# A four-layer graph network kernel: the loop without the transposes of Gd

## The chip, the cores and the metric

The kernel runs on one core of a Trainium2 chip. The metric is the device time of one execution in microseconds (us); less is better. The engines are TensorE (PE, with its weight loads as PEld), VectorE (DVE), ScalarE (ACT), GpSimd (POOL) and SyncE (SP), whose queue issues the DMAs.

## The reference

There are 128 graphs of 128 nodes with 256 features. Each passes four layers in turn, and after each layer the state is normalized over its features. The first layer is the one that the change touches (cut to its core):

```python
H = (adj != 0).astype(x.dtype)
w = adj.reshape(N, -1)[:, :C]
xw = einsum('ncd,hd->nch', x, W)
Dn = einsum('nce,ne->nc', H, w);  Dn = where(Dn > 0, 1.0 / Dn, 0.0)
Be = H.sum(axis=1);               Be = where(Be > 0, 1.0 / Be, 0.0)
m = Be[:, :, None] * einsum('nce,nch->neh', H, xw)
out = Dn[:, :, None] * einsum('nce,neh->nch', H, m) + b
# layer 1: y = conv(layer_norm(relu(conv(x, W1))), W2) + x;  x = layernorm(x + y)
# layer 2: x = layernorm(x + relu([x, adj @ x / deg] @ W));  layer 3: three GCN steps with adj
# layer 4: x = layernorm(x + relu((adj @ x) @ K) * (x has a nonzero))
```

So one convolution multiplies the state by diag(Dn) H diag(Be) H^T. The product G = H diag(Be) H^T is symmetric.

## The kernel before, in words

The work goes by pairs of graphs, 64 of them; g = 0, 1 is the graph in the pair, C = 128 the nodes, D = 256 the features. Each pair passes stages with short names, each a group of matmuls on PE and what the other engines do with its result. Products that need the full precision are taken as high and low parts (`_hi`, `_lo`): ACT rounds a value to its high part, and DVE or POOL subtracts that from the value to get the low part (`low_...` in the code); three matmuls then stand for one.

The stages of a pair around the change:

- `G(p)`: two matmuls make H diag(Be) H^T, the part with Be's high half in columns 0 to 127 and that with its low half in 128 to 255, and the degree Dn's sum in the last two columns.
- `scale_G(p)` on DVE: adds the two sums of the degree, inverts it (`dinv`, one number per node and graph, lying down the partitions), and makes Gd = dinv * (high half + low half), row by row, in three instructions: Gl (L1670), then Gd for each g (L1674).
- `Tr(p)` on PE (L417): two transposes of Gd, since the matmuls want it transposed. `copy_GT` on ACT copies the result from PSUM to GT, `round_GT` rounds it to GT_hi, and `low_GT` on POOL makes GT_lo.
- `Gx(p)`: GT by x. `R(p, 0)`, `R(p, 1)`: by W1. `P(p, 0)`, `P(p, 1)`: by W2, with `squares(p)` for the norm over the 512 hidden features. `square_mean`, `wide_var`, `root_h` and `make_p` (ACT, DVE, ACT, DVE) turn that norm into p; `round_p` and `low_p` split it. `GP(p)`: GT's parts by p's parts. `sum_n1` and `make_x1` then make the state of layer 2, which `xT` transposes.

The other stages (XAB, AXB; Ax2, H1, H1W, H2, H2W, AP3; Ax3, TK) are layers 2 to 4. Every engine runs one written list: `fill` for pairs 0 to 6, then `body(n)` for n = 7 to 61 (55 times), then `drain`. A body works on a different pair in each layer: n for G, Gd and Gx, n-1 for R, P and GP, n-2 to n-5 further down. On PE a body goes

```python
R(n-1,0) R(n-1,1) G(n) xT(n-2) H2W(n-4) Ax2(n-3) XAB(n-2) H1(n-3) AP3(n-4) P(n-1,0) P(n-1,1)
squares(n-1) Tr(n) AXB(n-2) H1W(n-3) Ax3(n-4) Gx(n) H2(n-3) GP(n-1) TK(n-4)
```

Nothing reorders this at run time: an instruction that waits on a semaphore holds all that stand behind it on its engine. SP's body loads the input of pair n+2 and stores the output of pair n-5, in that order. PSUM bank 0 is used by Ax2, Tr, H2 and R1 in turn.

Of the kernel before, what the change touches and what calls it, by code (L numbers as in the profile page):

```python
# [5 lines left out]
F32 = mybir.dt.float32  # L6
# [40 lines left out]
def build(nc, x, adjT, w1T, w2T, wab, v1, v2, v3, wk, columns, rows, eye, out):  # L47
# [5 lines left out]
    with ExitStack() as ctx:  # L53
# [70 lines left out]
        class Norm:  # L124
# [13 lines left out]
            def mv(self, p):  # L138
# [11 lines left out]
        table_loaded = sem("table_loaded")  # L150
        consts_step, beta_made, w1_hi, w1_lo, w2_scaled, w2_mean, w2_centred, w2c_hi, w2c_lo = (
            sem(s) for s in ("consts_step", "beta_made", "w1_hi", "w1_lo", "w2_scaled", "w2_mean",
                             "w2_centred", "w2c_hi", "w2c_lo"))
        betaW_made, wab_hi, wab_lo, v_hi, v_lo, b2_made = (
# [5 lines left out]
            sem(s) for s in ("ht_made", "ht_counted", "be_max", "be_made", "be_hi", "be_lo", "bh_high", "bh_made"))  # L160
        dn_0, dn_1, dn_2, dn_3, gl_made, gd_made = (sem(s) for s in ("dn_0", "dn_1", "dn_2", "dn_3", "gl_made", "gd_made"))
        w_hi, w_lo, gt_made, gx_hi, gx_lo = (sem(s) for s in ("w_hi", "w_lo", "gt_made", "gx_hi", "gx_lo"))
# [126 lines left out]
        def _(sp):  # L289
# [80 lines left out]
        def _(pe):  # L370
# [68 lines left out]
            def P(p, h):  # L439
                if p == 0 and h == 0:  # L440
                    pe.wait_ge(w2c_lo, 1)
# [154 lines left out]
            def fill():  # L596
# [10 lines left out]
                pe.wait_ge(gt_hi, 1)  # L607
                pe.wait_ge(w2_mean, 1)
                G(2)
# [174 lines left out]
            def body(n):  # L784
# [23 lines left out]
                squares(n - 1)  # L808
                pe.wait_ge(ax2_lo, n - 2)
                Tr(n)  # L810
                AXB(n - 2)
# [5 lines left out]
                Gx(n)  # L817
                pe.wait_ge(gt_hi, n + 1)
                H2(n - 3)
# [169 lines left out]
        def _(act):  # L989
# [63 lines left out]
            def copy_GT(p):  # L1053
                act.wait_ge(pe_did["Tr"], upto(p))
                if begun(p - 2):
                    act.wait_ge(pe_did["Gx"], upto(p - 2))
                    act.wait_ge(gt_lo, upto(p - 2))
                copy(GT[p % 2][:].rearrange("p a b -> p (a b)"),
                     psum[:, bank("Tr", p), 0:2 * C]).then_inc(gt_made, 1)

            def round_GT(p):
                if begun(p - 2):
                    act.wait_ge(pe_did["GP"], upto(p - 2))
                copy(GT_s[p % 2][0][:].rearrange("p a b -> p (a b)"),
                     psum[:, bank("Tr", p), 0:2 * C]).then_inc(gt_hi, 1)
# [136 lines left out]
            def round_w2():  # L1202
                act.wait_ge(w2_centred, 1)
                copy(w2c_s[0][:, :, 0:D], w2g[:]).then_inc(w2c_hi, 1)

# [178 lines left out]
            def body(n):  # L1384
# [178 lines left out]
        def _(dve):  # L1563
# [90 lines left out]
            def scale_G(p):  # L1654
                b = bank("G", p)
                both = slice(b[0], b[1] + 1, b[1] - b[0])
                dn = psum[:, b[1], 2 * C + 2:2 * C + 4]
                dve.wait_ge(pe_did["G"], upto(p))
                dve.tensor_reduce(dn, psum[:, both, 2 * C:2 * C + 2], AX_X, ALU.add).then_inc(dn_0, 1)
                dve.wait_ge(dn_0, upto(p))  # L1660
                dve.tensor_scalar(dn_max[:], dn, TINY, None, ALU.max).then_inc(dn_1, 1)
                dve.wait_ge(dn_1, upto(p))
                dve.reciprocal(dn_inv[:], dn_max[:]).then_inc(dn_2, 1)
                dve.wait_ge(dn_2, upto(p))
                dve.scalar_tensor_tensor(out=dinv[:], in0=dn, scalar=0.0, in1=dn_inv[:],
                                         op0=ALU.is_gt, op1=ALU.mult).then_inc(dn_3, 1)
                dve.wait_ge(dn_3, upto(p))
                if begun(p - 1):
                    dve.wait_ge(pe_did["Tr"], upto(p - 1))
                dve.tensor_tensor(Gl[:], psum[:, both, C:2 * C], bc(dinv[:], [C, 2, C], 2),  # L1670
                                  ALU.mult).then_inc(gl_made, 1)
                dve.wait_ge(gl_made, upto(p))
# [49 lines left out]
            def node_degree(p):  # L1722
                b = bank("AXB", p)
                dve.wait_ge(pe_did["AXB"], upto(p))
                dve.tensor_scalar(degm[:], psum[:, b:b + 2, D], DEG_EPS, None, ALU.max).then_inc(deg_max, 1)
                dve.wait_ge(deg_max, upto(p))
                dve.reciprocal(rdeg[:], degm[:]).then_inc(deg_inv, 1)

            def make_agg(p):
                b = bank("AXB", p)  # L1730
                dve.wait_ge(xa_out, upto(p))
                dve.wait_ge(deg_inv, upto(p))
# [37 lines left out]
            def mean_w2():  # L1770
                dve.wait_ge(pe_did["W2"], 1)
                dve.tensor_scalar(w2mean[:], psum[:, bank("W2", 0), 0:D], 1.0 / DH, None, ALU.mult).then_inc(w2_mean, 1)

            def centre_w2():
                dve.wait_ge(w2_mean, 1)
                dve.wait_ge(w2_scaled, KH)
                dve.tensor_tensor(w2g[:], w2g[:], bc(w2mean[:], [C, KH, D], 1), ALU.subtract).then_inc(w2_centred, 1)

            def high_w2():
                dve.wait_ge(w2_centred, 1)  # L1780
                dve.tensor_copy(w2c_s[0][:, :, 0:D], w2g[:]).then_inc(w2c_hi, 1)
# [408 lines left out]
        def _(pool):  # L2190
# [13 lines left out]
            def spread_low(p):  # L2204
# [107 lines left out]
            def body(n):  # L2312
# [98 lines left out]
```

## Time and profile before

| what | value |
|---|---|
| median of 3 runs | 1393.92 us (1392.55 to 1394.46) |
| the profiled execution's own time | 1393.31 us |
| its span, first to last instruction | 1391.2 us |
| around the span | 2.1 us |
| granted TensorE clock | 0.997 of full speed |
| busy: PE, DVE, ACT, POOL | 1376.9, 1134.6, 1122.7, 1003.6 us |
| DMA queue q1 | 44.91 MB, 10.1% of 16 engines |

The times of the rows below are taken from one body in the middle of the run (n is the same throughout) and are microseconds from the span's start. A matmul's length is from its start until its modelled end, and matmuls overlap, so the pace of PE is read from the distance between starts. A row's bracket gives the time its engine sat idle before it, and what ended that.

### The profile page before, as it was taken

To read this page: it belongs to the slowest core of one execution; us is meant where nothing else is said; L and a number is where in the kernel's file an instruction comes from. 1 tells how busy PE (TensorE), PEld (TensorE's weight loads), DVE (VectorE), ACT (ScalarE), POOL (GpSimd) and SP (SyncE) were. 2 spreads that over 40 slices of the span, in tenths; PEclk is the share of its full clock that TensorE was granted. 3 is DMA by queue.
4 is the path that set the end of the run, shared out by engine and by line. 5 is a ranking of instruction groups with operands and counts; after the bars stand their busy time and mean duration, and the time that the engine had idled before them with its cause. 6 is when DMAs were issued, how large, how long until landed. Compare 5 with 4: busy or idle time off the path is not lost.

```text
span 1391.2 us, 35333 instructions
## 1 busy us (share of the span) xinstructions
PE 1376.9 (99%) x10946; PEld 1335.9 (96%) x10946; DVE 1134.6 (82%) x4092; ACT 1122.7 (81%) x2639; POOL 1003.6 (72%) x1059
## 2 busy tenths in 40 slices
PE   8999999999999999999999999999999999999997
PEld 8999999999999999999999999999999999999996
DVE  7888788888887887788888878878888888888896
ACT  6777887887888878878878888888788788887776
POOL 5758778778778787787787787777877877877531
PEclk9999999999999999999999999999999999999999
DMA  4100110110100101101101101011011011010000
GB/s 143 36 20 20 40 39 20 39 40 20 39 29 31 39 21 39 39 20 40 39 20 40 32 28 39 21 39 39 21 39 39 20 40 37 23 40 21 8 22 34
DMA packets 29961, 47.17 MB, mean 34 GB/s; under 512 B 3408, under 2 KB 12240, under 8 KB 29776
## 3 DMA queue, kind: packets, MB, share of 16 engines
q1 hardware_dynamic: 29776, 44.91, 10.1%
q8 instruction: 90, 1.47, 0.4%
q14 instruction: 95, 0.78, 0.2%
HBM read 28.12 MB, written 16.78 MB: 32 GB/s over the span
## 4 chain that ended last, share of the span: by engine, by line
PE 98%; ACT 1%; issue 0%; DVE 0%; DMA 0%; SPq 0%; ACTq 0%; DVEq 0%
PE psum L374 95%; PE psum L473 2%; PE psum L417 1%; DMA n_s<-w2T_in 0%; ACT x L1010 0%; ACT tk L1172 0%; ACT h_hi L991 0%; DVE w2c_lo L1785 0%; DVE w2g L1767 0%; ACT w2c_hi L991 0%; ACT r_f L1015 0%; SPq L291 0%; ACT h_f L1015 0%; DVE n_st L1575 0%; DVE n_s L260 0%
## 5 line engine op out<-in xcount | busy, mean ns | idle before, releaser
L208 POOL TENSOR_TENSOR h_lo<-h_f,h_hi 128x512 fp32r<-128x512 f32 x120 | 154.9, 1291 | 93.6 <-ACT h_hi L991 93.4
L1010 ACT ACTIVATE x<-n_s,n_shift,n_rstd 128x256 f32<-128x256 f32 x384 | 208.0, 590 | 4.2 <-DVE n_shift L1599 4.1
L215 POOL TENSOR_TENSOR r_lo<-r_f,r_hi 128x512 fp32r<-128x512 f32 x123 | 158.7, 1292 | 44.1 <-ACT r_hi L991 43.9
L2229 POOL TENSOR_TENSOR n_s<-tk,mask 128x512 f32<-128x512 f32 x60 | 62.5, 1041 | 154.1 <-DVE mask L1652 133.0
L1575 DVE BATCH_NORM_STATS2 n_st<-n_s 128x6 f32<-128x256 f32 x384 | 141.9, 412 | 2.2
L374 PE MATMUL psum<-v_hi,h_hi 128*128 128x256 f32 x512 | 137.8, 292 | 2.0 <-ACT h_hi L991 2.0
L374 PE MATMUL psum<-A_f,x 128*128 128x128 f32 x1024 | 135.5, 275 | 0.6 <-ACT x L1010 0.5
L1015 ACT ACTIVATE h_f<-psum,columns 128x256 f32<-128x256 f32 x256 | 107.6, 472 | 34.8 <-PE psum L374 34.7
L374 PE MATMUL psum<-v_lo,h_hi 128*128 128x256 f32 x512 | 133.3, 282 | 0.0
L374 PE MATMUL psum<-gx_hi,w1T_hi 128*128 128x256 f32 x512 | 132.3, 281 | 0.0
L374 PE MATMUL psum<-gx_hi,w1T_lo 128*128 128x256 f32 x512 | 131.9, 281 | 0.0
L374 PE MATMUL psum<-w2c_hi,r_hi 128*128 128x258 f32 x512 | 129.5, 284 | 0.8 <-DVE w2c_lo L1785 0.8
L374 PE MATMUL psum<-w2c_lo,r_hi 128*128 128x258 f32 x512 | 129.4, 283 | 0.0
L374 PEld LDWEIGHTS psum<-A_f,x 128*128 128x128 f32 x1024 | 124.6, 191 | 1.6 <-ACT x L1010 1.1
L1005 ACT ACTIVATE n_std<-psum,eps_c 128x2 f32<-128x2 f32 x165 | 42.2, 256 | 93.5 <-DVE psum L1584 93.5
L208 DVE TENSOR_TENSOR ax_lo<-psum,ax_hi 128x512 fp32r<-128x512 f32 x128 | 88.5, 692 | 24.3 <-ACT ax_hi L991 21.1
L374 PE MATMUL psum<-wab_hi,x1T_hi 128*128 128x512 f32 x256 | 105.8, 413 | 0.0
L1015 ACT ACTIVATE r_f<-psum,columns 128x256 f32<-128x256 f32 x256 | 100.3, 469 | 5.9 <-PE psum L374 5.0
L374 PE MATMUL psum<-v_hi,h_lo 128*128 128x256 f32 x512 | 102.1, 281 | 0.0
L374 PE MATMUL psum<-gx_lo,w1T_hi 128*128 128x256 f32 x512 | 101.8, 281 | 0.0
L374 PE MATMUL psum<-wab_lo,x1T_hi 128*128 128x512 f32 x256 | 100.9, 394 | 0.0
L208 DVE TENSOR_TENSOR x1T_lo<-psum,x1T_hi 128x512 fp32r<-128x512 f32 x64 | 44.2, 691 | 69.3 <-ACT x1T_hi L991 69.3
(173 smaller groups left out, 5200.1 us busy)
## 6 DMA issues: line engine op xcount, KB each, us to landing
x_in<-x_in_dram SPq DMA_DIRECT2D x64, 256.0 KB, 2.8
out<-x SPq DMA_DIRECT2D x64, 256.0 KB, 2.0
at_in<-adjT SPq DMA_DIRECT2D x64, 128.0 KB, 2.2
x<-v_in SPq DMA_DIRECT2D x3, 256.0 KB, 5.7
n_s<-w2T_in SPq DMA_DIRECT2D x2, 256.0 KB, 3.3
r_f<-w1T_in SPq DMA_DIRECT2D x2, 256.0 KB, 5.1
h_f<-wab_in SPq DMA_DIRECT2D x2, 256.0 KB, 5.6
rows<-rows_in SPq DMA_DIRECT2D x1, 256.0 KB, 6.0
```

Source lines behind the costliest of these rows:

```text
L208: return e.tensor_tensor(dst[1][:], src, f(dst[0][:]), ALU.subtract).then_inc(signal, 1)
L215: e.tensor_tensor(r_s[1][:, half], r_f[:, half], f(r_s[0][:, half]), ALU.subtract).then_inc(r_lo[h], 1)
L374: return pe.matmul(o, a, b, start=start, stop=stop)
L417: last = pe.transpose(psum[:, bank("Tr", p), cols(g)], Gd[:, g, :], ident[:])
L473: last = pe.transpose(psum[:, bank("xT", p), (2 * m + g) * C:(2 * m + g + 1) * C], x1[p % 2][:, g, cols(m)], ident[:])
L1005: act.activation(nm.std[:], nm.mv(p)[:, :, 1], ACT.Sqrt, bias=eps_c[:, 0:1]).then_inc(nm.rooted, 1)
L1010: last = act.activation(dst[:, g, :], nm.s[:, g, :], ACT.Identity, scale=nm.rstd[:, g:g + 1], bias=nm.shift[:, g:g + 1])
L1015: return act.activation(dst[:, m].rearrange("p g c -> p (g c)"), psum[:, bank(stage, p), (m % 2) * 2 * C:(m % 2 + 1) * 2 * C], ACT.Relu, b ...
L1575: last = dve.bn_stats(nm.st[:, g, :], sum_in_psum(p, g) if nm is n1 else nm.s[:, g, :])
L2229: pool.tensor_tensor(n4.s[:], tk[:], bc(mask[:], [C, 2, D], 2), ALU.mult).then_inc(tk_masked, 1)
```

## The change

In the loop (pairs 7 to 61) the two transposes of Gd and ACT's copy of their result are gone. DVE adds the high and the low half of G in one reduction and doesn't scale it, so that Gd is symmetric and needs no transpose. The transposed scaled matrix has dinv along its columns, so dinv is needed as a row on every partition: SP stores dinv (128 x 2 numbers, 1 KB) to a small tensor in DRAM, waits until it has landed, and loads that row back to all 128 partitions (`dinv_b`, 1 KB each). POOL multiplies Gd by it and writes GT (`scale_GT`). ACT rounds GT from SBUF, ahead of `root_h` and no longer behind it. POOL's `low_GT` goes ahead of `make_xb`. Fill and drain keep the transposes. Several semaphores of steps that follow each other are merged into counters (`dn_step`, `deg_step`, `w2_step`); the order of those steps is the same.

```diff
--- before.py
+++ after.py
...
+        dinv_row = nc.dram_tensor("dinv_row", (C, 2), F32, kind="Internal").ap()
+        dinv_b = sb("dinv_b", [C, 2])
...
+        def in_loop(pair, lag):
+
+            return FIRST <= pair + lag < LAST
+
+        def spread(pair):
+
+            return 16 * (pair - FIRST + 1)
...
+            def spread_dinv(p):
+                sp.wait_ge(dinv_made, upto(p))
+                if in_loop(p - 1, 0):
+                    sp.wait_ge(dinv_spread, spread(p - 1))
+                sp.dma_start(dinv_row, dinv[:]).then_inc(dinv_stored, 16)
+                sp.wait_ge(dinv_stored, spread(p))
+                if in_loop(p - 1, 0):
+                    sp.wait_ge(gt_made, upto(p - 1))
+                sp.dma_start(dinv_b[:], dinv_row.partition_broadcast(C)).then_inc(dinv_spread, 16)
...
             def body(n):
                 if n + 2 < NP:
                     reload(n + 2)
+                if n < LAST:
+                    spread_dinv(n)
                 store(n - 5)
...
                 squares(n - 1)
-                pe.wait_ge(ax2_lo, n - 2)
-                Tr(n)
                 AXB(n - 2)
...
                 Gx(n)
-                pe.wait_ge(gt_hi, n + 1)
+                pe.wait_ge(ax2_lo, n - 2)
                 H2(n - 3)
...
             def round_GT(p):
                 if begun(p - 2):
                     act.wait_ge(pe_did["GP"], upto(p - 2))
+                if in_loop(p, 0):
+                    act.wait_ge(gt_made, upto(p))
+                    copy(GT_s[p % 2][0][:], GT[p % 2][:]).then_inc(gt_hi, 1)
+                    return
...
                 square_mean(n - 1)
-                copy_GT(n)
+                round_GT(n)
                 root_h(n - 1)
-                round_GT(n)
                 make_x3(n - 4)
...
                 dve.scalar_tensor_tensor(out=dinv[:], in0=dn, scalar=0.0, in1=dn_inv[:],
-                                         op0=ALU.is_gt, op1=ALU.mult).then_inc(dn_3, 1)
...
+                                         op0=ALU.is_gt, op1=ALU.mult).then_inc(dinv_made, 1)
+                if in_loop(p, 0):
+                    if in_loop(p - 1, 0):
+                        dve.wait_ge(gt_made, upto(p - 1))
+                    else:
+                        dve.wait_ge(pe_did["Tr"], turned(p - 1))
+                    dve.tensor_reduce(Gd[:], psum[:, both, 0:2 * C].rearrange("p g (h c) -> p g c h", h=2),
+                                      AX_X, ALU.add).then_inc(gd_made, 1)
+                    return
...
+            def scale_GT(p):
+                pool.wait_ge(gd_made, upto(p))
+                pool.wait_ge(dinv_spread, spread(p))
+                pool.wait_ge(gt_made, upto(p - 1))
+                pool.wait_ge(pe_did["Gx"], upto(p - 2))
+                pool.wait_ge(gt_hi, upto(p - 2))
+                pool.wait_ge(gt_lo, upto(p - 2))
+                pool.tensor_tensor(GT[p % 2][:], Gd[:], dinv_b[:].rearrange("p c g -> p g c"), ALU.mult).then_inc(gt_made, 1)
...
                 low_h1(pool, n - 3)
+                scale_GT(n)
                 if n + 1 < NP:
                     split_weights(n + 1)
                     spread_high(n + 1)
                     spread_low(n + 1)
+                low_GT(n)
                 make_xb(pool, n - 1)
-                low_GT(n)
                 low_p(pool, n - 1)
```

On POOL, in the second half of a body (GT is the scaled matrix, xb, p, x2c and h2 belong to other pairs), before:

```order
L208 TENSOR_TENSOR h1_lo<-h1_f,h1_hi 128x512 [waits h1_hi]
L2193 TENSOR_TENSOR BH<-at_in,BH 128x2 [waits w_hi]
L2196 TENSOR_TENSOR be_rest<-be_inv,be_r 128x2 [waits be_hi]
L2202 TENSOR_TENSOR BH<-HT,be_r 128x2x128 [waits pe_G,be_hi]
L2207 TENSOR_TENSOR BH<-HT,be_rest 128x2x128 [waits bh_high,be_lo]
L240 TENSOR_TENSOR xb<-x_in,b2half 128x512 [waits n1_summed,x_loaded0,b2_made]
L208 TENSOR_TENSOR GT1_lo<-GT1,GT1_hi 128x256 [waits pe_GP,gt_hi,gt_made]
L208 TENSOR_TENSOR p_lo<-p_f,p_hi 128x512 [waits pe_GP,p_hi]
```

and now:

```order
L222 TENSOR_TENSOR h1_lo<-h1_f,h1_hi 128x512 [waits h1_hi]
L2259 TENSOR_TENSOR GT0<-Gd,dinv_b 128x256 [waits pe_Gx,gt_hi,gt_made,gt_lo,dinv_spread,gd_made]
L2235 TENSOR_TENSOR BH<-at_in,BH 128x2 [waits w_hi]
L2238 TENSOR_TENSOR be_rest<-be_inv,be_r 128x2 [waits be_hi]
L2244 TENSOR_TENSOR BH<-HT,be_r 128x2x128 [waits pe_G,be_hi]
L2249 TENSOR_TENSOR BH<-HT,be_rest 128x2x128 [waits bh_high,be_lo]
L222 TENSOR_TENSOR GT0_lo<-GT0,GT0_hi 128x256 [waits pe_GP,gt_hi,gt_made]
L254 TENSOR_TENSOR xb<-x_in,b2half 128x512 [waits n1_summed,x_loaded1,b2_made]
L222 TENSOR_TENSOR p_lo<-p_f,p_hi 128x512 [waits pe_GP,p_hi]
```

One instruction of 128x256 came in between h1_lo and the four on BH, and GT_lo and xb changed places; p_lo stands behind all of them in both.

On ACT, between the squares of the wide norm and the rounding of p, before and then now:

```order
L1091 ACTIVATE h_mean<-psum 128x2
L991 ACTIVATE GT<-psum 128x256
L1095 ACTIVATE h_std<-h_veps 128x2
L991 ACTIVATE GT_hi<-psum 128x256
L1010 ACTIVATE x<-n_s,n_shift,n_rstd 128x256 x2
L991 ACTIVATE p_hi<-p_f 128x512
```

```order
L1122 ACTIVATE h_mean<-psum 128x2
L1015 ACTIVATE GT_hi<-GT 128x256
L1126 ACTIVATE h_std<-h_veps 128x2
L1034 ACTIVATE x<-n_s,n_shift,n_rstd 128x256 x2
L1015 ACTIVATE p_hi<-p_f 128x512
```

The copy GT is gone, and GT_hi, which now waits for POOL, stands ahead of h_std.

## Rows read from the trace of the kernel before

**Rows 1.** The page: busy time of each engine; the chain that ended last, by engine.

```profile
PE 1376.9 (99%) x10946; PEld 1335.9 (96%) x10946; DVE 1134.6 (82%) x4092; ACT 1122.7 (81%) x2639; POOL 1003.6 (72%) x1059
...
PE 98%; ACT 1%; issue 0%; DVE 0%; DMA 0%; SPq 0%; ACTq 0%; DVEq 0%
```

**Rows 2.** Timeline of SP's queue: start, length, engine, line, operation, out<-in.

```profile
691.49 0.34 SPq L311 DMA_DIRECT2D out<-x  x1
...
733.92 0.34 SPq L311 DMA_DIRECT2D out<-x  x1
```

**Rows 3.** Timeline of PE and its weight loads: xT; squares, Tr, AXB; GP.

```profile
693.81 0.60 PE L473 MATMUL psum<-ident,x 128*128 128x128 f32 x4
...
694.37 0.28 PE L374 MATMUL psum<-v_lo,h_hi 128*128 128x256 f32 x1
...
704.40 0.50 PE L374 MATMUL psum<-ones,sq 128*128 128x1 f32 x4
704.76 0.42 PE L417 MATMUL psum<-ident,Gd 128*128 128x128 f32 x2
...
705.14 0.28 PE L374 MATMUL psum<-xbw_hi,A_lo 128*128 128x258 f32 x1
705.26 0.29 PE L374 MATMUL psum<-xbw_hi,A_hi 128*128 128x258 f32 x1
...
708.06 1.06 PE L374 MATMUL psum<-GT,x_in 128*128 128x128 f32 x8
...
709.97 0.19 PEld L374 LDWEIGHTS psum<-p_lo,GT_hi 128*128 128x128 f32 x1
```

**Rows 4.** Timeline of DVE: x1 for xT, dinv, Gl and Gd, a reduction.

```profile
692.11 1.00 DVE L1613 TENSOR_SCALAR x<-psum,n_mv,n_rstd 128x256 f32<-128x256 f32 x2
...
698.71 0.16 DVE L1665 SCALAR_TENSOR_TENSOR dinv<-psum,dn_inv 128x2 f32<-128x2 f32 x1
698.90 0.42 DVE L1670 TENSOR_TENSOR Gl<-psum,dinv 128x256 f32<-128x256 f32 x1
699.36 0.61 DVE L1674 SCALAR_TENSOR_TENSOR Gd<-psum,dinv,Gl 128x128 f32<-128x128 f32 x2
...
700.20 0.42 DVE L1685 TENSOR_REDUCE ht_count<-HT 128x2 f32<-128x256 f32 x1
```

**Rows 5.** Landing of the stores (L311), of the at_in loads (L291), and one broadcast load.

```profile
DMA to landing us min/median/max: 2.0/2.0/3.4
...
DMA to landing us min/median/max: 1.9/2.2/5.4
...
rows<-rows_in SPq DMA_DIRECT2D x1, 256.0 KB, 6.0
```

**Rows 6.** Timeline of POOL, the second half of the body.

```profile
702.66 1.30 POOL L208 TENSOR_TENSOR h_lo<-h_f,h_hi 128x512 fp32r<-128x512 f32 x1
703.91 0.20 POOL L2193 TENSOR_TENSOR BH<-at_in,BH 128x2 fp32r<-128x2 f32 x1
...
706.80 0.73 POOL L208 TENSOR_TENSOR GT_lo<-GT,GT_hi 128x256 fp32r<-128x256 f32 x1
707.59 1.28 POOL L208 TENSOR_TENSOR p_lo<-p_f,p_hi 128x512 fp32r<-128x512 f32 x1
708.82 1.29 POOL L2222 TENSOR_TENSOR x2c<-x,rows 128x512 f32<-128x512 f32 x1
711.63 1.29 POOL L208 TENSOR_TENSOR h_lo<-h_f,h_hi 128x512 fp32r<-128x512 f32 x1 [1.52 <-ACT h_hi L991]
```

**Rows 7.** Timeline of ACT from the wide norm's squares on.

```profile
704.94 0.17 ACT L1091 ACTIVATE h_mean<-psum 128x2 f32<-128x2 f32 x1
705.22 0.39 ACT L991 ACTIVATE GT<-psum 128x256 f32<-128x256 f32 x1
705.54 0.20 ACT L1095 ACTIVATE h_std<-h_veps 128x2 f32<-128x2 f32 x1
705.65 0.37 ACT L991 ACTIVATE GT_hi<-psum 128x256 fp32r<-128x256 f32 x1
```

More of the change, by code:

```diff
@@ L150, in build @@
         table_loaded = sem("table_loaded")
-        consts_step, beta_made, w1_hi, w1_lo, w2_scaled, w2_mean, w2_centred, w2c_hi, w2c_lo = (
-            sem(s) for s in ("consts_step", "beta_made", "w1_hi", "w1_lo", "w2_scaled", "w2_mean",
-                             "w2_centred", "w2c_hi", "w2c_lo"))
+        consts_step, beta_made, w1_hi, w1_lo, w2_scaled, w2_step = (
+            sem(s) for s in ("consts_step", "beta_made", "w1_hi", "w1_lo", "w2_scaled", "w2_step"))
         betaW_made, wab_hi, wab_lo, v_hi, v_lo, b2_made = (
@@ L160, in build @@
             sem(s) for s in ("ht_made", "ht_counted", "be_max", "be_made", "be_hi", "be_lo", "bh_high", "bh_made"))
-        dn_0, dn_1, dn_2, dn_3, gl_made, gd_made = (sem(s) for s in ("dn_0", "dn_1", "dn_2", "dn_3", "gl_made", "gd_made"))
+        dn_step, dinv_made, gl_made, gd_made = (sem(s) for s in ("dn_step", "dinv_made", "gl_made", "gd_made"))
+        dinv_stored, dinv_spread = sem("dinv_stored"), sem("dinv_spread")
         w_hi, w_lo, gt_made, gx_hi, gx_lo = (sem(s) for s in ("w_hi", "w_lo", "gt_made", "gx_hi", "gx_lo"))
@@ L166, in build @@
         hm2, hv, hve, hstd, hrstd = (sem(s) for s in ("h_mean2", "h_var", "h_veps", "h_std", "h_rstd"))
-        deg_max, deg_inv = sem("deg_max"), sem("deg_inv")
+        deg_step = sem("deg_step")
         p_made, p_hi, p_lo, xb_made = sem("p_made"), sem("p_hi"), sem("p_lo"), sem("xb_made")
@@ L192, in bank, with turned @@
             return BANK_OF.get((stage, pair), BANK[stage])
+        def in_loop(pair, lag):
+            return FIRST <= pair + lag < LAST
+        def spread(pair):
+            return 16 * (pair - FIRST + 1)
+        def turned(pair):
+            return pair + 1 if pair < FIRST else FIRST + max(0, pair - LAST + 1)
         def inputs(p):
@@ L440, in P @@
                 if p == 0 and h == 0:
-                    pe.wait_ge(w2c_lo, 1)
+                    pe.wait_ge(w2_step, 4)
                 outs = [(psum[:, bank("P", p) + g, 0:D + 2],
@@ L607, in fill @@
                 pe.wait_ge(gt_hi, 1)
-                pe.wait_ge(w2_mean, 1)
+                pe.wait_ge(w2_step, 1)
                 G(2)
@@ L1053, in copy_GT @@
             def copy_GT(p):
-                act.wait_ge(pe_did["Tr"], upto(p))
+                act.wait_ge(pe_did["Tr"], turned(p))
+                if in_loop(p - 1, 0):
+                    act.wait_ge(gt_made, upto(p - 1))
                 if begun(p - 2):
@@ L1057, in copy_GT @@
                     act.wait_ge(gt_lo, upto(p - 2))
+                    act.wait_ge(gt_hi, upto(p - 2))
                 copy(GT[p % 2][:].rearrange("p a b -> p (a b)"),
@@ L1202, in round_w2 @@
             def round_w2():
-                act.wait_ge(w2_centred, 1)
-                copy(w2c_s[0][:, :, 0:D], w2g[:]).then_inc(w2c_hi, 1)
+                act.wait_ge(w2_step, 2)
+                copy(w2c_s[0][:, :, 0:D], w2g[:]).then_inc(w2_step, 1)
             def fill():
@@ L1658, in scale_G @@
                 dve.wait_ge(pe_did["G"], upto(p))
[L1659 to L1664, printed above, removed]
-                dve.scalar_tensor_tensor(out=dinv[:], in0=dn, scalar=0.0, in1=dn_inv[:],
-                                         op0=ALU.is_gt, op1=ALU.mult).then_inc(dn_3, 1)
@@ L1667, in scale_G @@
-                dve.wait_ge(dn_3, upto(p))
+                dve.tensor_reduce(dn, psum[:, both, 2 * C:2 * C + 2], AX_X, ALU.add).then_inc(dn_step, 1)
+                dve.wait_ge(dn_step, 3 * p + 1)
+                dve.tensor_scalar(dn_max[:], dn, TINY, None, ALU.max).then_inc(dn_step, 1)
+                dve.wait_ge(dn_step, 3 * p + 2)
+                dve.reciprocal(dn_inv[:], dn_max[:]).then_inc(dn_step, 1)
+                dve.wait_ge(dn_step, 3 * p + 3)
+                if p > FIRST and in_loop(p - 1, 0):
+                    dve.wait_ge(dinv_stored, spread(p - 1))
@@ new lines, in scale_G @@
+                dve.scalar_tensor_tensor(out=dinv[:], in0=dn, scalar=0.0, in1=dn_inv[:],
+                                         op0=ALU.is_gt, op1=ALU.mult).then_inc(dinv_made, 1)
+                if in_loop(p, 0):
+                    if in_loop(p - 1, 0):
+                        dve.wait_ge(gt_made, upto(p - 1))
[4 more added lines that the diff above has]
+                    return
@@ L1668, in scale_G @@
+                dve.wait_ge(dinv_made, upto(p))
                 if begun(p - 1):
-                    dve.wait_ge(pe_did["Tr"], upto(p - 1))
+                    dve.wait_ge(pe_did["Tr"], turned(p - 1))
+                if in_loop(p - 1, 0):
+                    dve.wait_ge(gt_made, upto(p - 1))
                 dve.tensor_tensor(Gl[:], psum[:, both, C:2 * C], bc(dinv[:], [C, 2, C], 2),
                                   ALU.mult).then_inc(gl_made, 1)
-                dve.wait_ge(gl_made, upto(p))
+                dve.wait_ge(gl_made, turned(p))
@@ L1724, in node_degree @@
                 dve.wait_ge(pe_did["AXB"], upto(p))
-                dve.tensor_scalar(degm[:], psum[:, b:b + 2, D], DEG_EPS, None, ALU.max).then_inc(deg_max, 1)
-                dve.wait_ge(deg_max, upto(p))
-                dve.reciprocal(rdeg[:], degm[:]).then_inc(deg_inv, 1)
+                dve.tensor_scalar(degm[:], psum[:, b:b + 2, D], DEG_EPS, None, ALU.max).then_inc(deg_step, 1)
+                dve.wait_ge(deg_step, 2 * p + 1)
+                dve.reciprocal(rdeg[:], degm[:]).then_inc(deg_step, 1)
             def make_agg(p):
@@ L1731, in make_agg @@
                 dve.wait_ge(xa_out, upto(p))
-                dve.wait_ge(deg_inv, upto(p))
+                dve.wait_ge(deg_step, 2 * p + 2)
                 for g in range(2):
@@ L1771, in mean_w2 @@
                 dve.wait_ge(pe_did["W2"], 1)
-                dve.tensor_scalar(w2mean[:], psum[:, bank("W2", 0), 0:D], 1.0 / DH, None, ALU.mult).then_inc(w2_mean, 1)
+                dve.tensor_scalar(w2mean[:], psum[:, bank("W2", 0), 0:D], 1.0 / DH, None, ALU.mult).then_inc(w2_step, 1)
             def centre_w2():
-                dve.wait_ge(w2_mean, 1)
+                dve.wait_ge(w2_step, 1)
                 dve.wait_ge(w2_scaled, KH)
-                dve.tensor_tensor(w2g[:], w2g[:], bc(w2mean[:], [C, KH, D], 1), ALU.subtract).then_inc(w2_centred, 1)
+                dve.tensor_tensor(w2g[:], w2g[:], bc(w2mean[:], [C, KH, D], 1), ALU.subtract).then_inc(w2_step, 1)
             def high_w2():
-                dve.wait_ge(w2_centred, 1)
-                dve.tensor_copy(w2c_s[0][:, :, 0:D], w2g[:]).then_inc(w2c_hi, 1)
+                dve.wait_ge(w2_step, 2)
+                dve.tensor_copy(w2c_s[0][:, :, 0:D], w2g[:]).then_inc(w2_step, 1)
             def low_w2():
-                dve.wait_ge(w2c_hi, 1)
+                dve.wait_ge(w2_step, 3)
                 dve.tensor_tensor(w2c_s[1][:, :, 0:D], w2g[:], f(w2c_s[0][:, :, 0:D]),
-                                  ALU.subtract).then_inc(w2c_lo, 1)
+                                  ALU.subtract).then_inc(w2_step, 1)
             def spread_beta():
```

## The prediction

> **What bounds the kernel now.** I read the page first. PE is busy for 99% of the span, and the chain that ended last lies on PE for 98% [rows 1]. So PE is the bound, it is hardly ever kept waiting, and a microsecond off its list is a microsecond off the time, as long as what it waits for comes as early as it does now. The next view is the timeline of SP's queue, for the length of a body: two bodies lie between the two stores, (733.92 - 691.49) / 2 = 21.215 us [rows 2], and 55 of them are 1167 us of the span. Then come the timelines of the engines within that one body, and in them two things: how long a slot the transposes hold on PE, and how far ahead of PE each engine is where the change touches it. The times below are those of that body. PE's times behind the removed slot are read as earlier by the length of the slot.
>
> **What PE loses.** A transposes' row is 0.42 us long, but matmuls overlap, so I go by starts [rows 3]. Tr starts at 704.76. The second matmul of AXB starts at 705.14 and the third at 705.26, a pace of 0.12, so that the first one's turn was 705.02. The slot of Tr is 705.02 - 704.76 = 0.26 us. A second reading: the four transposes of xT start at 693.81 and the second matmul behind them at 694.37; with one pace off, 694.25, that makes 0.44 us for four, or 0.22 for two. I take 0.26, as it is read at the seam that the change closes; 0.22 is the low end, and the 0.42 of the row itself the far one. The loop runs 55 bodies: 55 x 0.26 = 14.3 us (12.1 by the low end, 23.1 by the far one). Fill and drain keep their transposes, nine pairs of them.
>
> **What DVE does.** Gl and two Gd are 0.42 + 0.61 us [rows 4] and go. In their place stands one reduction that reads 512 numbers per partition from PSUM and writes 256. The nearest row is the reduction that reads 256 in 0.42 us [rows 4]; twice the read is at most 0.84, and the start-up counted once makes it nearer 0.7. Either way it isn't longer than the 1.07 us from 698.90 to the end of Gd at 699.97, so DVE gains 0.2 to 0.4 us there. That time is given back at the latest where DVE waits for the squares of the wide norm, which PE makes before the removed slot. I count it as nothing, and if the reduction were as long as what it replaces it would still cost nothing.
>
> **What ACT does.** Its copy of GT, 0.39 us, goes. GT_hi (0.37 from PSUM) is now read from SBUF and goes ahead of h_std. h_mean ends at 705.11, and h_std started at 705.54 [rows 7]. If GT is there by 705.1, GT_hi fills just that gap and h_std starts within 0.05 us of where it did. Cost nothing, with the gap as its cover.
>
> **The new path of dinv, the part that decides.** dinv is there at 698.71 + 0.16 = 698.87 [rows 4]. SP has issued its loads of this body at about 692 (its store at 691.49 is the first of the three in a row [rows 2]), so it is free and waits for dinv. The store of this body comes 14 us later, so the two new DMAs hold up nothing on SP, and they add 55 x 1 KB written and 55 x 128 KB read to queues that are busy for a tenth. The trace has no DMA of 8 bytes per partition. The nearest rows are the output's stores, 2.0 us to landing at the least and in the median, 3.4 at the most, and, for the load of 1 KB to each of 128 partitions, at_in's, which have just that shape: 1.9, 2.2 and 5.4 [rows 5]. The one broadcast load took 6.0 [rows 5], but among all the weight loads of the fill. I take 2.0 + 2.2 and 0.1 for the hand-overs (an estimate): dinv_b lands at 703.2. Both ends: 2.0 + 1.9 makes 702.9, and 3.4 + 5.4 makes 707.8.
>
> The multiplication on POOL stands behind h_lo, which ends at 703.96 [rows 6]. So POOL comes to it 0.75 us after the row has landed, and doesn't wait. Its size is that of GT_lo, two full inputs of 128x256, 0.73 us [rows 6]; what differs is that one input is read with a step of two numbers. I take 0.73. GT is then there at 704.7, in time for ACT (705.1) and far ahead of Gx, at 708.06 - 0.26 [rows 3].
>
> All that stands behind it on POOL is later by 0.73: the four on BH (needed in the next body), GT_lo and xb (the swap of the two changes nothing for a third), and then p_lo. Now GT_lo ends at 707.53 and p_lo starts at 707.59. It will start near 708.26 and end, as 1.23 us lie between its start and that of x2c, at 709.5. PE loads the weights for the first matmul that takes p_lo at 709.97 [rows 3], which becomes 709.71. So 0.2 us are left of what were 1.1. This is the thinnest place of the forecast: p_lo on POOL is what is late next. Behind it POOL has 1.52 us idle before h_lo at 711.63 [rows 6], so the addition doesn't carry over into the next body.
>
> The other chain that could be late next is h_std, p_f, GP, x1, xT. x1 ends at 693.11 and xT starts at 693.81 [rows 3, 4]: 0.70 us of slack, of which the shorter body takes 0.26. It holds unless h_std is late by over 0.44.
>
> **The sum.** 1393.31 - 14.3 = 1379.0 for the profiled execution. The median of the runs is 0.6 above it, so 1379.6 us against 1393.92.
>
> **A rule that speaks against it.** The stores that the trace shows landed in 2.0 us whatever their place in the run [rows 5], but none of them is of small pieces. The Trainium skill, DMA: Bandwidth & Descriptors (Specifications, and Anatomy of one DMA), says that pieces under 512 B make the DMA engine read, modify and write, and that most of the roughly 2 us of a DMA is the wait for the write's receipt, "surprisingly long" where the target is HBM. By it the first hop here, 8 bytes each into DRAM, could be the dear one. The fixed 2 us agrees with the rows; what small pieces add no row shows. A second rule bears on POOL: the skill's GPSIMD Engine Reference (Performance pitfalls for Q7 kernels) has reads with a step of over 8 bytes cost half as much again. The step here is exactly 8 bytes, so by the rule there is no surcharge; if the edge fell on the other side, 0.37 us more would leave a stall of 0.17 us a body, and the sum would be 1389.
>
> **The rivals.** A stall of PE at p_lo comes back in every body. With d the time by which the multiplication ends later than 704.7, it is d - 0.2, and the change breaks even at d = 0.46.
>
> A (part of the gain goes at p_lo). POOL's multiplication takes longer or the row lands slightly late, d between 0.3 and 0.6: for 0.4, 55 x (0.26 - 0.2) = 3.3 us gained, 1390.6; over the span of d, 1385 to 1402. For it: 0.2 us is thin, and the two DMAs have no row of their own. Against it: 0.75 us of reserve stands before the multiplication.
>
> B (slower: the two hops through DRAM). The small store lands like the slowest store, 3.4 us, and the load in 2.2: dinv_b at 704.57 and d = 0.6, so 55 x (0.4 - 0.26) = 7.7 us lost, 1401.6. The point from which it decides: two hops that take over 5.45 us together. If the store takes twice the usual 2.0, d is 1.2 and the time 1435. For it: the small pieces. Against it: the median of the stores is their minimum, that of the loads 0.3 us above theirs [rows 5], and the queues are nearly empty at 699 to 703.
>
> C (no change: something else holds PE). The late row makes GT_hi late, and with it h_std and x1; from the numbers above that begins only at d = 0.85, later than p_lo does, so it only adds to B. Another form is that the seam between squares and AXB keeps its slot, since the 0.26 us also hide the way from squares of one kind of matmul to the next: 1393.9. Against it: the four transposes of xT with the way over to H2W in them came to 0.11 us each [rows 3], so a change of kind costs no slot there.
>
> **Chances.** Forecast 0.60, A 0.18 (half of it still faster by over 0.2%), B 0.16, C 0.06. A measurement of this kernel can't tell less than 0.2%, or 2.8 us, from no change. Faster 0.68, within 0.2% 0.11, slower 0.21. The range goes from 1376.5, a slot of 0.32 us, to 1402, which takes in A and the near end of B; beyond lies the rest of B. The forecast's own range is 1376.5 to 1382.
>
> **What would show it.** In the profile after: bodies of 20.95 us by SP's stores; squares followed by AXB with no row between; the two new DMAs issued near 698.9 and 701 on this body's scale, with landings of about 2 us each; POOL's multiplication right behind h_lo with no idle before it and 0.73 us long; no PE or PEld wait for POOL's p_lo. If POOL shows idle before the multiplication ended by the DMA, the path of dinv is too long; if the multiplication is over 0.95 us long, POOL is the cause. Either then shows as idle time of PE ahead of the p_lo matmuls in each body, and makes the prediction wrong.

## The result, and the profile after

The changed kernel takes 1471.51 us in the median of 4 runs (1471.21 to 1472.64) against 1393.43 us, a ratio of 1.0562 (95% interval 1.0543 to 1.0580). It is 78 us slower, where 14 us less were forecast, and it lies outside the range. The profiled span is 1469.4 us, at a granted clock of 0.998.

The page after, engines and the chain that ended last, as [rows 1] of before:

```profile
PE 1391.9 (95%) x10836; PEld 1329.8 (90%) x10836; DVE 1125.4 (77%) x3982; ACT 1111.0 (76%) x2584; POOL 1036.3 (71%) x1114
...
PE 51%; DMA 26%; ACT 9%; DVE 5%; issue 5%; POOL 3%; ACTq 0%; SPq 0%; POOLq 0%; DVEq 0%
PE psum L400 49%; DMA dinv_b<-dinv_row 15%; DMA dinv_row<-dinv 11%; ACT x L1034 4%; POOL GT L2259 3%; DVE ax_lo L222 3%; ACT ax_hi L1015 2%; PE psum L499 2%; ACT r_hi L1015 2%; DVE dn_inv L1693 1%; ACT h_std L1126 1%; DVE dinv L1697 1%; DVE dn_max L1691 1%; DMA r_f<-w1T_in 0%; DVE psum L1689 0%
```

The chain lay on PE for 98% before. Now half of it is off PE, and the two new DMAs alone are 26%. The view of waits after (engine and line, what it waited for, us in total, times, the longest) names the carriers:

```profile
POOL GT L2259 <- DMA dinv_b<-dinv_row: 110.7, 55, 2.8
...
ACT GT_hi L1015 <- POOL GT L2259: 87.7, 55, 2.4
PEld psum L400 <- ACT x L1034: 72.8, 56, 2.1
...
PEld psum L400 <- POOL p_lo L222: 11.5, 51, 0.5
```

The first three occur in every one of the 55 bodies, the last in 51. Now the landing of the two DMAs after, first the load of the row (L335), then the store of dinv (L331), to be held against [rows 5]:

```profile
DMA to landing us min/median/max: 2.9/4.0/5.0
...
DMA to landing us min/median/max: 2.5/2.8/4.2
```

One body of the timeline after, SP, DVE and POOL, as [rows 2, 4, 6]:

```profile
712.69 0.33 SPq L331 DMA_DIRECT2D dinv_row<-dinv  x1
715.54 0.33 SPq L335 DMA_DIRECT2D dinv_b<-dinv_row  x1
...
712.50 0.16 DVE L1697 SCALAR_TENSOR_TENSOR dinv<-psum,dn_inv 128x2 f32<-128x2 f32 x1
712.58 0.68 DVE L1704 TENSOR_REDUCE Gd<-psum 128x256 f32<-128x512 f32 x1
...
716.37 1.29 POOL L222 TENSOR_TENSOR h_lo<-h_f,h_hi 128x512 fp32r<-128x512 f32 x1
719.46 0.74 POOL L2259 TENSOR_TENSOR GT<-Gd,dinv_b 128x256 f32<-128x256 f32 x1 [1.80 <-DMA dinv_b<-dinv_row]
...
723.71 1.28 POOL L222 TENSOR_TENSOR p_lo<-p_f,p_hi 128x512 fp32r<-128x512 f32 x1
```

POOL is ready for the row at 717.66 and stands idle for 1.80 us; the mean of all bodies is 110.7 / 55 = 2.01 us. The same body on ACT and PE, as [rows 7, 3]:

```profile
718.74 0.17 ACT L1122 ACTIVATE h_mean<-psum 128x2 f32<-128x2 f32 x1
720.30 0.42 ACT L1015 ACTIVATE GT_hi<-GT 128x256 fp32r<-128x256 f32 x1 [1.39 <-POOL GT L2259]
720.62 0.19 ACT L1126 ACTIVATE h_std<-h_veps 128x2 f32<-128x2 f32 x1
720.72 1.07 ACT L1034 ACTIVATE x<-n_s,n_shift,n_rstd 128x256 f32<-128x256 f32 x2
...
718.20 0.50 PE L400 MATMUL psum<-ones,sq 128*128 128x1 f32 x4
718.56 0.37 PE L400 MATMUL psum<-xbw_hi,A_hi 128*128 128x258 f32 x1
718.77 0.28 PE L400 MATMUL psum<-xbw_hi,A_lo 128*128 128x258 f32 x1
...
721.85 1.16 PE L400 MATMUL psum<-A_f,x 128*128 128x128 f32 x8 [0.90 <-ACT x L1034]
...
725.04 0.19 PEld L400 LDWEIGHTS psum<-p_lo,GT_hi 128*128 128x128 f32 x1 [0.22 <-POOL p_lo L222]
```

ACT waits 1.39 us for GT. Behind GT_hi stand h_std and then x3 (the row L1034), which needs nothing of it, and PE waits for x3 at Ax3. A second, small wait comes at p_lo. A body is now 22.66 us on the mean of the 54 distances between the stores of dinv, against 21.22: 55 x 1.45 = 79 us.

### The profile page after: what moved, and what is told of

It reads as the page before. It is cut to its first block, busy times and chain, and to the rows that moved or that the text cites. A ratio compares the mean times of both kernels' runs of the same rounds, so it can differ in the third digit from the quotient of the medians.

```text
span 1469.4 us, 35338 instructions
## 1 busy us (share of the span) xinstructions
PE 1391.9 (95%) x10836; PEld 1329.8 (90%) x10836; DVE 1125.4 (77%) x3982; ACT 1111.0 (76%) x2584; POOL 1036.3 (71%) x1114
## 4 chain that ended last, share of the span: by engine, by line
PE 51%; DMA 26%; ACT 9%; DVE 5%; issue 5%; POOL 3%; ACTq 0%; SPq 0%; POOLq 0%; DVEq 0%
PE psum L400 49%; DMA dinv_b<-dinv_row 15%; DMA dinv_row<-dinv 11%; ACT x L1034 4%; POOL GT L2259 3%; DVE ax_lo L222 3%; ACT ax_hi L1015 2%; PE psum L499 2%; ACT r_hi L1015 2%; DVE dn_inv L1693 1%; ACT h_std L1126 1%; DVE dinv L1697 1%; DVE dn_max L1691 1%; DMA r_f<-w1T_in 0%; DVE psum L1689 0%
## 5 line engine op out<-in xcount | busy, mean ns | idle before, releaser
L1034 ACT ACTIVATE x<-n_s,n_shift,n_rstd 128x256 f32<-128x256 f32 x384 | 207.7, 589 | 4.3 <-DVE n_shift L1629 4.1
L400 PE MATMUL psum<-A_f,x 128*128 128x128 f32 x1024 | 141.0, 281 | 61.8 <-ACT x L1034 61.6
L400 PEld LDWEIGHTS psum<-A_f,x 128*128 128x128 f32 x1024 | 124.4, 191 | 73.2 <-ACT x L1034 72.8
L2259 POOL TENSOR_TENSOR GT<-Gd,dinv_b 128x256 f32<-128x256 f32 x55 | 40.9, 744 | 110.7 <-DMA dinv_b<-dinv_row 110.7
```

The costliest lines, as they stand in the source:

```text
L400: return pe.matmul(o, a, b, start=start, stop=stop)
L1034: last = act.activation(dst[:, g, :], nm.s[:, g, :], ACT.Identity, scale=nm.rstd[:, g:g + 1], bias=nm.shift[:, g:g + 1])
L2259: pool.tensor_tensor(GT[p % 2][:], Gd[:], dinv_b[:].rearrange("p c g -> p g c"), ALU.mult).then_inc(gt_made, 1)
```

## The experiments

Every kernel differs from the changed one only by the edit shown. e1, e2 and e11 show the calls of a body in their order (cut to those that matter); the other edits are cut to their core. e1 to e4 ran on one chip, e5 to e8 on a second and e9 to e11 on a third. The kernel before took 1394.0, 1393.5 and 1394.1 us there, so their times can be compared. The hops differ more, as the table further down shows.

**e1, both queues in another order.**

```diff
-  ACT:  square_mean  round_GT  root_h  make_x3  round_p  copy_h1w
+  ACT:  square_mean  root_h  make_x3  round_p  copy_h1w  round_GT
-  POOL: low_h1  scale_GT  split_weights  spread_high  spread_low  low_GT  make_xb  low_p
+  POOL: low_h1  split_weights  spread_high  spread_low  make_xb  scale_GT  low_p  low_GT
```

> The changed kernel with POOL's multiplication moved behind the four on BH and xb, and GT_lo behind p_lo, and ACT's GT_hi moved behind x3, p_hi and h1w. The two DMAs are as they are. Theory (the hops take 6.8 us, and only what stands behind the waiting instructions makes that cost): the row lands before POOL comes to it, no wait there, x3 and p_lo in time, bodies of 21.05 us, 1384 us. Rival (the DMAs themselves or POOL's added 0.74 us hold PE up, whatever the order): 1440 or more.

Measured: 1383.74 us in 5 runs, ratio 0.9929 (0.9917 to 0.9941). It is 10 us (0.7%) faster than the kernel before. In the timeline of e1, POOL, there is no idle time before the multiplication:

```profile
700.31 1.30 POOL L254 TENSOR_TENSOR xb<-x_in,b2half 128x512 f32<-128x512 f32 x1
701.64 0.74 POOL L2259 TENSOR_TENSOR GT<-Gd,dinv_b 128x256 f32<-128x256 f32 x1
702.46 1.28 POOL L222 TENSOR_TENSOR p_lo<-p_f,p_hi 128x512 fp32r<-128x512 f32 x1
```

Bodies are 21.05 us on the mean. The two hops took even longer, 3.1 and 4.4 us in the median, so with the same hops the order decides whether they cost anything.

**e2, ACT's order alone.**

```diff
-  ACT:  square_mean  round_GT  root_h  make_x3  round_p  copy_h1w
+  ACT:  square_mean  root_h  make_x3  round_p  copy_h1w  round_GT
```

> The changed kernel with ACT's GT_hi alone moved behind x3, p_hi and h1w; POOL as it is. Theory of two chains (x3 behind GT_hi on ACT, and p_lo behind the multiplication on POOL, about equally late): PE no longer waits for x3, but 1.3 us a body for p_lo instead of 0.2, and the time stays at 1466 to 1472 us. Rival (x3 is the one chain): 0.2 us a body of waiting at p_lo is left, 1396 us.

Measured: 1538.81 us, ratio 1.1041 (1.1026 to 1.1056). The place is as the theory of two chains said: PE's wait for x3 is gone, and p_lo holds PE in every body. The size is not. The waits of e2:

```profile
POOL GT L2259 <- DMA dinv_b<-dinv_row: 144.7, 55, 3.1
...
PE psum L400 <- POOL p_lo L222: 109.1, 55, 2.3
```

Two things add to the 1.3 us expected. The hops took 3.1 and 4.4 us here, not 2.8 and 4.0, so POOL idled for 2.6 us a body and not 2.0, and PE waited 2.0 us for p_lo. And TensorE's clock fell behind this wait in some bodies. The timeline of e2, PE, shows two of these waits:

```profile
735.68 0.39 PE L400 MATMUL psum<-p_lo,GT_hi 128*128 128x256 f32 x1 [1.68 <-POOL p_lo L222]
...
758.84 0.39 PE L400 MATMUL psum<-p_lo,GT_hi 128*128 128x256 f32 x1 [1.86 <-POOL p_lo L222]
```

The windows of e2 (us, each engine's busy time and instructions in it, the granted clock, DMA share, GB/s), around the second of them:

```profile
748.00:760.00 12.00, 10.14 (x86) 9.94 (x86) 9.04 (x34) 8.52 (x21) 9.35 (x13) 1.00 0.15 14
760.00:764.00 4.00, 4.00 (x23) 4.00 (x22) 3.54 (x16) 1.76 (x4) 1.27 (x2) 0.57 0.53 164
764.00:776.00 12.00, 12.00 (x93) 11.44 (x92) 7.69 (x26) 8.86 (x20) 8.88 (x8) 1.00 0.09 3
```

The clock is full until 760, mostly at the lower level (1.2 of 2.4 GHz) for about 3.4 of the next 4 us, and full again. This body is 24.66 us from store to store of dinv, where the one before, with a wait of 1.68 us, is 22.99. Of the 54 distances, 33 lie between 22.9 and 23.8 and 21 between 24.6 and 25.2. A body less its wait is 21.3 us in the mean of the 33 and 22.8 in that of the 21, so the clock's price is about 1.5 us in two bodies of five. The length of the wait doesn't tell which: one of 2.30 us left the clock full (timeline of e2, PE, and its windows):

```profile
235.60 0.39 PE L400 MATMUL psum<-p_lo,GT_hi 128*128 128x256 f32 x1 [2.30 <-POOL p_lo L222]
...
235.00:241.00 6.00, 5.40 (x46) 5.40 (x47) 3.91 (x16) 3.54 (x10) 3.21 (x4) 1.00 0.39 113
```

**e3, the row taken out of the path.** The first layer is scaled by another pair's degrees.

```diff
-        dinv_b = sb("dinv_b", [C, 2])
+        dinv_b = [sb(f"dinv_b{b}", [C, 2]) for b in range(2)]
-                pool.wait_ge(dinv_spread, spread(p))
+                pool.wait_ge(dinv_spread, spread(max(p - 1, FIRST)))
# the DMA writes dinv_b[p % 2], scale_GT(p) reads dinv_b[max(p - 1, FIRST) % 2]
```

> The changed kernel with two buffers for the spread row, and POOL multiplying by the row of the pair before (so the first layer is scaled by another pair's degrees); both DMAs are still made in each body, nothing waits for the one of this body. Theory (the hops' latency on the path is the whole loss): multiplication right behind h_lo, no waits for x3 or p_lo beyond 0.1 us, bodies of 21.05 us, 1384 us. Rival (part of the loss is POOL's added work or the DMAs' traffic): over 1390, with a wait at p_lo.

Measured: 1384.76 us, ratio 0.9937 (0.9921 to 0.9952), bodies of 21.08 us. With the changed order and both DMAs kept, the loss is gone. Neither POOL's added 0.74 us nor the traffic costs more than the 1 us by which e3 is above e1. The timeline of e3, POOL and PEld, shows the reserve that p_lo has when nothing is late:

```profile
705.38 1.28 POOL L222 TENSOR_TENSOR p_lo<-p_f,p_hi 128x512 fp32r<-128x512 f32 x1
...
707.09 0.19 PEld L400 LDWEIGHTS psum<-p_lo,GT_hi 128*128 128x128 f32 x1
```

p_lo ends at 706.66, 0.43 us ahead of the load of its weights, and nearly all bodies of e3 have the same.

**e8, p_lo ahead of GT_lo on POOL**, and nothing else.

```diff
-                low_GT(n)
                 make_xb(pool, n - 1)
                 low_p(pool, n - 1)
+                low_GT(n)
```

> The changed kernel with POOL's p_lo moved ahead of GT_lo alone; ACT as it is, so x3 still stands behind GT_hi. Theory of two chains in a row (x3 costs 1.1 us a body and p_lo 0.2 more): p_lo's wait goes, x3's stays, 1455 to 1462 us. Rival (p_lo is the chain that counts, as predicted): the waits shrink by all of the 0.7 us that p_lo gains, 1433 us or less.

Measured: 1461.60 us, ratio 1.0486 (1.0466 to 1.0506). This is as the theory said. PE waits for p_lo once (0.2 us); the wait of its weight loads for x3 is 76.9 us against 72.8. So in the changed kernel x3 holds PE first, and p_lo takes only what is left over.

**e11, POOL's order alone.**

```diff
-  POOL: low_h1  scale_GT  split_weights  spread_high  spread_low  low_GT  make_xb  low_p
+  POOL: low_h1  split_weights  spread_high  spread_low  make_xb  scale_GT  low_p  low_GT
```

> The changed kernel with POOL alone in the order of e1 (multiplication behind xb, GT_lo behind p_lo), and ACT as it is, with GT_hi ahead of h_std and x3. Theory (ACT's queue behind the waiting GT_hi is a chain of its own): GT comes 1 us later than in the changed kernel, x3 and Ax3 with it, PE waits over 2 us at one place in each body, and its clock falls to the lower level behind some of these waits as in e2: 1500 to 1560 us. Rival (x3's wait grows by 1.0 us and p_lo's 0.2 goes, the clock stays): 1510 or so with a granted clock of 0.99 or more. Rival (POOL's order is the cure, ACT's isn't needed): 1384 to 1395 us.

Measured: 1539.11 us, ratio 1.1040 (1.1022 to 1.1059), granted clock 0.971. This is as the theory said. Of the 54 distances, 31 are 23.2 to 23.4 us and 23 are 24.8 to 24.9. The waits of e11:

```profile
ACT GT_hi L1015 <- POOL GT L2259: 133.1, 55, 2.6
PEld psum L400 <- ACT x L1034: 118.1, 56, 2.3
```

POOL doesn't wait for the row here in any body. GT is late because POOL comes to it later, and ACT's queue hands that on to x3. The wait of PE is nearly the same in all bodies, and the clock falls behind some. The timeline of e11, PE, shows two, and the windows of e11 the stretches behind them:

```profile
1283.86 2.00 PE L400 MATMUL psum<-A_f,x 128*128 128x128 f32 x8 [1.93 <-ACT x L1034]
1308.72 1.16 PE L400 MATMUL psum<-A_f,x 128*128 128x128 f32 x8 [1.93 <-ACT x L1034]
...
1284.00:1290.00 6.00, 6.00 (x39) 6.00 (x40) 4.75 (x14) 3.78 (x8) 3.19 (x3) 0.72 0.01 3
1308.00:1314.00 6.00, 5.28 (x46) 5.28 (x47) 5.79 (x17) 5.21 (x12) 3.92 (x4) 1.00 0.00 0
```

The first of these bodies is 24.85 us long and the second 23.24, so here a fall of the clock costs 1.6 us.

e1, e2 and e11 together: putting one queue right leaves the other to hold PE up, and the longer single wait makes it dearer through the clock; both together remove the loss.

**e4, e5, e6, e7, e9, e10, the hops by themselves.** In all of them the first layer is scaled by other numbers than its degrees. What each DMA's other end was changed to (first hop: `dinv_row <-`; second: `dinv_b <-`):

```diff
# e4:  first hop as it is                     second: adjT[p], 128 different KB
# e5:  first hop as it is                     second: rows[0], one KB never written, 128 times
# e6:  no first hop (nor its wait)            second: adjT[p]
# e7:  at_in[0:1, p % RING], one partition    second as it is, the row just written
# e9:  no first hop (nor its wait)            second: rows[0]
# e10: at_in[0:1, p % RING], one partition    second: adjT[p]
```

> The changed kernel with the second DMA reading 128 different KB of DRAM (the pair's adjacency, so the first layer is scaled by other numbers) in place of one KB 128 times; the first hop and all waits are the same. Theory (the many reads of one KB make the load 4.0 us where at_in's takes 2.2): landing in 2.2 us, the row there 1.8 us earlier, POOL waits 0.1 us or less, 1385 us. Rival (the load is slow because it follows a store, or for its place in the body): landing stays near 4.0 us, 1471 us.

> The changed kernel with the second DMA reading the one KB of an input that no one writes (b2's row, so the first layer is scaled by other numbers), 128 times as before; the first hop and all waits are the same. Theory (many reads of one KB are what makes the load slow; with 128 different KB it landed in 3.1 us): landing 4.0 to 4.4 us and 1465 to 1475 us. Rival (it is slow because it reads what a store has just written): landing 3.1 us or less, about 1440 us.

> The changed kernel without the store of dinv, and with the load from 128 different KB (so the first layer is scaled by other numbers): one hop in place of two. Either theory of the hops: the load alone lands by 702 us on the scale of the body shown, before POOL comes to it, no wait of POOL, 1384 us. Rival (anything else in the changed order costs time): over 1390. What it also tells: if the load lands in 2.2 us as at_in's, the store ahead of it was what made it 3.1; if it stays at 3.1, its place in the body is.

> The changed kernel with the first hop storing one KB of one partition (of the adjacency, so the first layer is scaled by other numbers) in place of 8 bytes of each of 128; the second hop is the broadcast of that row as before. Theory (small pieces make the store 2.8 us where the output's stores take 2.0): landing 2.0 to 2.2 us, some 0.7 us earlier on the path, 1435 us. Rival (the store's time doesn't depend on its pieces): landing 2.8 to 3.1, 1471 us.

> The changed kernel without the store of dinv, and with the load reading the one KB of an input 128 times (so the first layer is scaled by other numbers). With 128 different KB and no store ahead it landed in 2.0 us. Theory A (the store of small pieces right ahead is what adds 0.9 us to either source): 2.0 us here too. Theory B (reading one KB 128 times adds 0.9 us by itself): 2.9 us. The time is 1382 to 1384 us by both, as POOL comes to the row later than it lands.

> The changed kernel with the first hop storing one KB of one partition, and the second reading 128 different KB (so the first layer is scaled by other numbers). With the row just written as the source this store was followed by a load of 2.9 us. Theory A (a load right behind any store is slower by 0.9 us): 2.9 us. Theory B (reading one KB 128 times is slower, a store of one piece ahead does nothing): 2.0 us. The time is 1382 to 1384 us by both.

Landing of the second hop (median, with the extremes where they are wide), and the kernel's time in one run:

| first hop | 128 different KB | one KB, never written | the row just written |
|---|---|---|---|
| none | 2.0 (e6: 1382.41) | 2.9 (e9: 1383.98) | |
| one partition's KB | 2.0 (e10: 1383.75) | | 2.9 (e7: 1383.54) |
| 8 bytes of 128 partitions | 3.1, 2.0 to 4.5 (e4: 1442.04) | 2.9 (e5: 1425.28) | 4.0 (the changed kernel: 1471.51) |

Two of the rows behind it, e6's load and e9's:

```profile
DMA to landing us min/median/max: 1.9/2.0/3.2
...
DMA to landing us min/median/max: 2.8/2.9/3.1
```

Reading one KB 128 times costs 0.9 us over reading 128 different ones, with nothing ahead of it (e9 against e6). A store of one piece ahead adds nothing (e10, e7). A store of small pieces ahead adds 1.1 us to the load of what it wrote (changed kernel against e7), nothing to that of another KB (e5), and to 128 others something between nothing and 2.5 us (e4). e4 ran on the chip on which both hops were longer in all kernels: the first took 3.1 to 3.2 us in e1 to e4, and 2.8 to 2.9 in the changed kernel, e5, e8 and e11; the load of the row just written took 4.4 in e1 to e3, and 4.0 to 4.1 in the others. So e4's 3.1 is to be held against 4.4, and how much of its 1.1 us over e6 comes from the store is not known. My expectation for e4, that reading one KB so often was the whole surplus, was wrong by half, and in e5 both sides were wrong: the load was as quick as the rival said, and the time 15 us under its number, which was e4's time; the first hop took 2.8 us there and 3.2 in e4. The first hop by itself is the clearest: SP issues the second DMA 1.11 us behind the first in e7, in the timeline of e7,

```profile
714.79 0.24 SPq L331 DMA_DIRECT2D dinv_row<-at_in  x1
715.90 0.34 SPq L335 DMA_DIRECT2D dinv_b<-dinv_row  x1
```

where 8 bytes of each of 128 partitions took 2.8. (The trace lists no landing for this store, so it is the distance at which SP went on; it is 1.10 to 1.13 us in all bodies.) Theory and rival of e7 were both off: one piece is far quicker than the 2.0 us of the output's stores. e7 changed two things at once, the size of the pieces and the number of partitions read, and no run separates them.

## Why the prediction was wrong, point by point

- **The bound and its reading** held: PE's list set the time before, and in e1 and e3 each microsecond off it came out.
- **The slot** was mis-sized. 0.26 us was forecast. From the first matmul of squares to the second of AXB it was 0.74 us [rows 3] and is 0.57 after: 0.17 us saved. The forecast put the turn of AXB's first matmul one pace of 0.12 us ahead of the second, at 705.02. The rows of before, PE, have it earlier, and the same for H2W behind xT:

```profile
694.17 0.37 PE L374 MATMUL psum<-v_hi,h_hi 128*128 128x256 f32 x1
...
704.94 0.36 PE L374 MATMUL psum<-xbw_hi,A_hi 128*128 128x258 f32 x1
```

  From start to start Tr held 704.94 - 704.76 = 0.18 us, and the four transposes of xT 694.17 - 693.81 = 0.36, or 0.18 for two. The first matmul of a new kind is followed by the next only after 0.20 us, in both kernels (718.56 to 718.77 after). So the size stood in the trace before. Bodies of 21.05 us in e1 confirm it: 55 x 0.165 = 9 us, and e1 gains 10.
- **DVE** held: the reduction took 0.68 us where 0.7 to 0.84 were worked out, and its gain of 0.2 us was given back in a wait for PE (0.25 us before n_s at 715.50 in the body shown). **ACT's own term** held in size, 0.42 us for GT_hi.
- **The hops** are the step that failed: "I take 2.0 + 2.2 and 0.1 for the hand-overs". Measured were 2.8 + 4.0, so the row landed 1.8 us behind POOL's arrival in the body shown (2.0 on the mean) and not 0.75 us ahead of it. The shape of the destination was taken as what sets the load's time, and the rows of large stores as what sets the small one's. The experiments show what was left out: the load takes 0.9 us more for reading one KB 128 times (e9 against e6) and 1.1 more behind the store of small pieces (against e7), and the store of one row takes 1.1 us where this one took 2.8 (e7).
- **The multiplication on POOL** held: 0.74 us for 0.73, with its step of 8 bytes.
- **"p_lo on POOL is what is late next"** was half right. It is p_lo's reserve that sets the size of the loss, but 0.2 us was too little: e3 shows 0.43. With the mean wait of POOL, PE's stall is 2.01 - 0.43 = 1.58 us; less the 0.165 of the slot that is 1.42 a body, 78 us, as measured. The same sum gives 50 us for e4 (POOL waited 82.5 / 55 = 1.50 us), where 48 were lost, and 32 for e5 (65.1 / 55 = 1.18), where 32 were. The forecast's own d - 0.2 gives 1472 us with the wait of the body shown, d = 1.80, but that is luck: this body's wait is below the mean, and with the mean it would be 1484.

  And PE spends most of the stall earlier, at Ax3. The sentence that ACT's order costs nothing until d = 0.85 overlooked x3, which stands behind h_std. GT was to be there 0.4 us before ACT needs it, and in the timeline of before x3 ended at 706.99 for an Ax3 that began at 707.17, 0.18 us more; so x3 is late from d = 0.6 on (an estimate):

```profile
705.91 1.08 ACT L1010 ACTIVATE x<-n_s,n_shift,n_rstd 128x256 f32<-128x256 f32 x2
...
707.17 1.05 PE L374 MATMUL psum<-A_f,x 128*128 128x128 f32 x8
```

  e8, in which x3 alone holds PE, bears this out: POOL waits 2.1 us a body, and its bodies are 22.43 us, 1.4 over those of e1, which makes a reserve of 0.7 us. The omission changed the place and not the size, since p_lo is late by a little more (e8 got only 10 us back).
- **Rival B** named the mechanism, its point of decision (5.45 us for both hops; they took 6.8) and the skill's rule. Its chance of 0.16 was too low, and it priced the first hop alone. The rule of the Trainium skill, DMA: Bandwidth & Descriptors (Specifications), on pieces under 512 B agrees with the trace in its direction: 2.8 us with pieces of 8 bytes, 1.1 with one row. That the engine's reading, modifying and writing is the reason, no run shows. The fixed 2 us, which the Trainium skill, DMA: Bandwidth & Descriptors (Anatomy of one DMA), gives for the path by way of GpSimd, doesn't hold for that one row from SP's queue: into the same DRAM tensor it took 1.1 us. That the load behind it pays as well, 4.0 against 2.9 us, stands on no row of before.
- **Rival A's** form, a POOL late by its own work, did not occur (e3). Of **rival C**, the late GT_hi came, but by way of x3; a seam that keeps the whole slot did not, though it kept 0.09 us of the 0.26.

Open are why the load is slower behind a store of small pieces (the table tells which loads are, not by what), whether it is the size or the number of the pieces that makes that store slow, and why the hops took 0.3 to 0.4 us longer on the chip of e1 to e4. The order in the kernel is not the reason: e4, with the longer first hop, has the order of the changed kernel, and e11, with the shorter hops, has that of e1 on POOL.

## What to carry to other kernels

A wait put into a queue is priced by its latency less the reserve of everything behind it on that queue, and such a wait can sit on two engines at once: freeing one of them can show nothing or even cost more (e2, e11). Where a value goes by way of DRAM, take the time of each hop from a DMA with the same source, the same destination and the same size of pieces. If the trace has none, leave room (here the hops took 1.6 times the estimate), and put the consumer where the queue has other work; here the same two hops cost 78 us or nothing, and removing the transposes was worth 10 us only in the second order.

## What the runs showed of the hardware that was not expected

- A store of 1 KB as 8 bytes from each of 128 partitions took 2.8 us, and from one partition 1.1 us, until SP went on.
- A load of one KB to 128 partitions took 2.9 us from one KB and 2.0 us from 128 different KB.
- The same idle time of PE, 1.93 us in one piece, was followed in e11 by the lower clock in 23 of 54 bodies and by the full clock in 31, at a price of 1.6 us each. In e2 the shortest wait followed by a fall was 1.86 us, while one of 2.30 us was followed by none. What decides between the two, no run shows.
- The changed kernel's waits of 0.8 to 1.8 us left the clock full; one body, with a wait of 1.91 us, had a fall (24.84 us long, where the others are 22.4 to 23.3).
